# Gate and up products of a feed-forward layer by seven block products in place of eight

## The chip, the cores and the metric

The kernel runs on one core of one Trainium2 chip. The metric is the device time of one execution in microseconds (us). Before the change it is 2055.05 us, the median of three runs (2053.92 to 2055.37).

## The reference, cut to what matters

One cross-attention layer and one gated feed-forward layer, each with a layer norm ahead and a residual sum behind. The first takes 1190 us of the span and is not changed. The second works on 1600 tokens (16 x 100) of width 512 and a hidden width of 4096, with 4-bit weight codes and one scale per 32 inputs:

```python
xt = layernorm(x).reshape(1600, 512)
Wg, Wu, Wd = (lut[codes] * scales for gate, up, down)       # (4096, 512), (4096, 512), (512, 4096)
gate = einsum('th,nh->tn', xt, Wg)
up   = einsum('th,nh->tn', xt, Wu)
gelu = tanh(0.79788 * (gate + 0.044715 * gate**3)) * gate * 0.5 + gate * 0.5
out  = x + einsum('tn,hn->th', gelu * up, Wd)
```

## The kernel before, in words

Every float32 operand of a large product is kept as a pair of rounded halves (`_hi`, `_lo`), and a product is three matmuls: hi x hi, lo x hi, hi x lo (`matmul3`, L318 for each of them). A `_hi` half is made by a cast on ScalarE (L660), the `_lo` half by a subtraction on VectorE (L891) or GpSimd.

The feed-forward hidden width is cut into `JT` = 16 slices of 256 columns (index jt), the tokens into `NCHUNK` = 4 chunks of 400 (index ch). One step m is one slice and one chunk:

- `gate_up(m)`: for each half z of 128 hidden columns, `half(m, z, 0)` (gate) and `half(m, z, 1)` (up), 12 matmuls of 128x400 each over four blocks of 128 inputs: 48 matmuls. n = 2m + z numbers the halves.
- per n: ScalarE squares the gate values out of PSUM (L780) and scales them (L782), VectorE multiplies by the gate (`argument`, L1089), ScalarE takes tanh (L788), VectorE does `gelu` (L1097) and `gated` (L1104), each with one operand in PSUM; ScalarE casts `inter_hi` (L660), GpSimd subtracts `inter_lo` (L1357).
- `down(m)`: four output blocks of 6 matmuls, 24 in all, each added to the residual sum in SBUF by VectorE (`down_add`, L1118).

TensorE issues gate_up(m), then down(m-1), 72 matmuls a step. Gate and up use PSUM banks 0 to 3, down uses banks 4 to 7. Each engine works through its own list in order and waits on semaphores.

The codes of the next slice are turned into weights meanwhile, in six pieces of 128x512 (gate, up, down, two nibbles each): VectorE `decode` (two TENSOR_SCALAR, L1075 and L1077, and one TENSOR_TENSOR, L1080, all SBUF to SBUF in int16), GpSimd `decode_scaled` (L1339), ScalarE `decode_hi` (L660), GpSimd `decode_lo` (L1346). `decode` of a piece waits until `decode_scaled` of the piece two before is done, since there are two `value` buffers. `pieces_at` sets the place of each piece in the steps. The weights of two slices have room side by side.

## Time and profile before

| | |
|---|---|
| median of three runs | 2055.05 us |
| profiled execution: its time | 2053.49 us |
| profiled execution: span | 2051.7 us |
| TensorE busy | 2022.6 us (99%) |
| VectorE busy | 1420.0 us (69%) |
| ScalarE busy | 967.8 us (47%) |
| GpSimd busy | 913.8 us (45%) |
| granted TensorE clock, mean | 0.998 |

Times in the profile are microseconds from the span's start. A busy time of TensorE is made of matmuls that overlap: one of 128x400 is listed with about 0.34 us, but the next starts 0.18 us after it. For how fast TensorE works, starts are compared, not durations. In the rows PE is TensorE, DVE is VectorE, ACT is ScalarE, POOL is GpSimd, and L318 is line 318 of the kernel.

### The profile page before, as it was taken

The numbers are of one execution on the slowest core, as the hardware profiler recorded it, in microseconds if no ns is written. First come the engines' busy times: TensorE is split into PE (matmuls) and PEld (weight loads), VectorE is DVE, ScalarE is ACT, GpSimd is POOL, SyncE is SP. The second block draws the span as 40 slices with busy tenths as digits, with TensorE's granted clock in tenths as the row PEclk, the third lists the DMA queues.
The fourth block names the chain that finished last, engine by engine and source line by source line (L and its number), as shares of the span: only waits on it lengthen the run. The fifth ranks groups of instructions, "written<-read, shape, count | busy, mean of one in ns | idle before, by whom it ended". The sixth has DMA issues, their size and how long they took to land.

```text
span 2051.7 us, 33236 instructions
## 1 busy us (share of the span) xinstructions
PE 2022.6 (99%) x11840; PEld 1951.7 (95%) x11840; DVE 1420.0 (69%) x2938; ACT 967.8 (47%) x2126; POOL 913.8 (45%) x1041
## 2 busy tenths in 40 slices
PE   6999999999999999999999999999999999999999
PEld 5899999999999999999999999999999999999999
DVE  6777777778877787877887977555555555555554
ACT  4555455555555555555555544333333333333332
POOL 6756655533444333344233345444444444444441
PEclk9999999999999999999999999999999999999999
DMA  6335344332333324233233241001000000000001
GB/s 185 131 108 171 124 132 130 129 107 87 128 107 96 126 86 140 84 112 118 81 111 116 95 160 45 31 32 31 32 31 31 32 31 32 31 31 31 1 1 65
DMA packets 91763, 172.05 MB, mean 84 GB/s; under 512 B 13056, under 2 KB 48016, under 8 KB 89552
## 3 DMA queue, kind: packets, MB, share of 16 engines
q1 hardware_dynamic: 91600, 169.93, 25.3%
q8 instruction: 96, 1.57, 0.3%
q14 instruction: 67, 0.55, 0.1%
HBM read 136.55 MB, written 33.36 MB: 83 GB/s over the span
## 4 chain that ended last, share of the span: by engine, by line
PE 94%; DVE 3%; ACT 1%; POOL 1%; issue 1%; DMA 0%; SPq 0%; POOLq 0%; DVEq 0%; ACTq 0%
PE psum L318 70%; PE psum L351 6%; PE psum L383 3%; PE psum L375 3%; PE psum L398 3%; PE psum L404 3%; PE psum L399 3%; PE psum L448 2%; DVE kaT_lo L891 1%; PE psum L414 1%; DVE work L997 0%; PE psum L419 0%; DMA xb<-in_x 0%; DVE yT_lo L891 0%; DVE k_ss L947 0%
## 5 line engine op out<-in xcount | busy, mean ns | idle before, releaser
L1089 DVE TENSOR_TENSOR sq<-psum,sq 128x400 f32<-128x400 f32 x128 | 73.5, 574 | 266.9 <-ACT sq L782 266.9
L891 DVE TENSOR_TENSOR kaT_lo<-psum,kaT_hi 128x488 fp32r<-128x488 f32 (+2 forms) x384 | 216.0, 613 | 51.8 <-ACT kaT_hi L660 51.8
L720 ACT ACTIVATE work<-psum,stats,q_rstd 100x361 f32<-100x361 f32 x256 | 163.8, 651 | 184.1 <-DVE stats L988 184.1
L318 PE MATMUL psum<-wk,ctxT_hi 128*122 128x512 f32 x768 | 242.8, 398 | 2.2 <-DVE wk L891 2.2
L1357 POOL TENSOR_TENSOR inter_lo<-act,inter_hi 128x400 fp32r<-128x400 f32 x128 | 136.9, 1070 | 186.9 <-ACT inter_hi L660 186.9
L660 ACT CAST kaT_hi<-psum 128x488 fp32r<-128x488 f32 (+2 forms) x384 | 178.9, 539 | 73.3 <-PE psum L383 72.3
L1276 POOL TENSOR_TENSOR k_ss<-k_ss,power 122x4 f32<-122x4 f32 x192 | 194.0, 1010 | 16.0
L978 DVE TENSOR_REDUCE stats<-psum 100x2 f32<-100x722 f32 x128 | 115.7, 904 | 106.1 <-PE psum L351 106.1
L780 ACT ACTIVATE sq<-psum 128x400 f32<-128x400 f32 x128 | 64.7, 505 | 247.8 <-PE psum L318 247.8
L318 PE MATMUL psum<-xT_hi,up_lo 128*128 128x400 f32 x512 | 176.9, 346 | 0.0
L318 PE MATMUL psum<-xT_hi,gate_hi 128*128 128x400 f32 x512 | 176.2, 344 | 0.7 <-DVE act L1104 0.7
L318 PE MATMUL psum<-xT_lo,up_hi 128*128 128x400 f32 x512 | 176.6, 345 | 0.0
L318 PE MATMUL psum<-xT_lo,gate_hi 128*128 128x400 f32 x512 | 176.6, 345 | 0.0
L318 PE MATMUL psum<-xT_hi,gate_lo 128*128 128x400 f32 x512 | 176.5, 345 | 0.0
L318 PE MATMUL psum<-inter_lo,down_hi 128*128 128x400 f32 x512 | 176.0, 344 | 0.0
L318 PE MATMUL psum<-xT_hi,up_hi 128*128 128x400 f32 x512 | 176.0, 344 | 0.0
L318 PE MATMUL psum<-inter_hi,down_lo 128*128 128x400 f32 x512 | 175.6, 343 | 0.0
L318 PE MATMUL psum<-inter_hi,down_hi 128*128 128x400 f32 x512 | 174.9, 342 | 0.0
L318 PEld LDWEIGHTS psum<-wk,ctxT_hi 128*122 128x122 f32 x768 | 140.2, 184 | 34.1 <-issue 2.4
L1274 POOL TENSOR_SCALAR k_ss<-k_ss 122x4 f32<-122x4 f32 x192 | 37.3, 195 | 300.4 <-DVE k_ss L947 299.7
L318 PE MATMUL psum<-xlnT_hi,head_w 128*128 128x400 f32 x512 | 150.1, 354 | 3.0 <-DVE xlnT_lo L891 1.8
L318 PE MATMUL psum<-wk,ctxT_lo 128*122 128x512 f32 x384 | 152.1, 396 | 0.0
(146 smaller groups left out, 5580.2 us busy)
## 6 DMA issues: line engine op xcount, KB each, us to landing
head_w<-spill_sq SPq DMA_DIRECT2D x48, 512.0 KB, 3.4
head_w<-spill_so SPq DMA_DIRECT2D x46, 512.0 KB, 3.8
wk<-spill_sk SPq DMA_DIRECT2D x12, 1024.0 KB, 5.2
wv<-spill_sv SPq DMA_DIRECT2D x48, 256.0 KB, 2.8
spill_sq<-head_w SPq DMA_DIRECT2D x16, 512.0 KB, 3.0
spill_so<-head_w SPq DMA_DIRECT2D x16, 512.0 KB, 3.0
wk_raw<-in_ctxT SPq DMA_DIRECT2D x12, 361.0 KB, 4.0
head_raw<-in_Wq SPq DMA_DIRECT2D x16, 256.0 KB, 3.7
```

The costliest lines, as they stand in the source:

```text
L318: last = e.matmul(out, a_, b_, start=i == 0, stop=i == len(passes) - 1)
L351: last = e.matmul(bank[3 + h][0:SQ, 0:SCOLS], qT[quad % 2][h][q_][:, qs], kT[k_][:, h, 0:SCOLS], start=term == 0, stop=term == 2)
L375: last = e.transpose(bank[t][:, cols(h, KP)], khat[:, t, cols(h, HD)], ident[0:KP, 0:KP])
L383: last = e.transpose(bank[3 + t][0:KN[t], cols(h, SQ)], attn[h][:, t * KP:t * KP + KN[t]], ident[0:SQ, 0:SQ])
L660: e.copy(dst, src).then_inc(S[sem], 1)
L720: e.activation(attn[h][:, 0:SKV], bank[3 + h][0:SQ, 0:SKV], ACT.Exp, bias=st[:, h:h + 1], scale=rq[:, i * QH + h:i * QH + h + 1], accum_ou ...
L780: e.activation(sq[:, :], gate_bank(n), ACT.Square, scale=1.0 / CODE).then_inc(S["g2"], 1)
L891: e.tensor_tensor(dst, src, high.bitcast(F32), ALU.subtract).then_inc(S[sem], 1)
L978: e.tensor_reduce(st[:, 2 * p:2 * p + 2], scored(p), AX_X, ALU.max, negate=True).then_inc(S["mx"], 1)
L1089: e.tensor_tensor(sq[:, :], gate_bank(n), sq[:, :], ALU.mult).then_inc(S["arg"], 1)
L1276: e.tensor_tensor(c, c, power[0:KP, :], ALU.pow).then_inc(S["krs"], 1)
L1357: e.tensor_tensor(il[:, :], gact[n % 2][:, :], ih[:, :].bitcast(F32), ALU.subtract).then_inc(S["il"], 1)
```

## The change

Slice 0 is computed as before. For the 15 other slices two chunks of tokens are taken together as a pair p (h = p % 2 is 0 for chunks 0 and 1, 1 for chunks 2 and 3; two pairs a slice). The product of gate (and of up) is seen as 2x2 blocks: two halves of the hidden columns, two halves of the inputs, two chunks. Seven block products of 6 matmuls give what eight gave. They use sums of weight blocks (S1 to S4, made anew for every slice) and sums of token blocks (T1 to T4, made once and kept in SBUF). Three PSUM banks for gate and three for up (roles a, b, c) gather them; two are left for down, used in turn.

```diff
+PAIRS = 2 * (JT - 1)
+PRODUCTS = (("a", "A11", "B11"), ("b", "A12", "B21"), ("a", "S2", "T2"), ("c", "S1", "T1"), ("a", "S3", "T3"),
+            ("c", "S4", "B22"), ("a", "A22", "T4"))
...
+            def product(p, k, i):
...
+                if i == 0:
+                    e.wait_ge(S["gelu" if k == 0 else "inter"], before + 1 if p > 0 else (7, 8)[k])
...
+                elif i == 1 and k == 0:
+                    e.wait_ge(S["gelu"], before + 3)
...
+                elif i == 6:
+                    e.wait_ge(S[("gadd", "uadd")[k]], 3 * p + 2)
...
+            for p in range(PAIRS):
+                for at in range(2 * NP):
+                    product(p, at % 2, at // 2)
+                    if p == 0 and 3 <= at < 7:
+                        down(12 + at - 3)
+                    elif p > 0 and 3 <= at < 11:
+                        down(8 + 8 * p + at - 3)
```

TensorE adds each product into a bank (`role_bank`). ScalarE copies a running bank out (`evict`, six copies a pair), VectorE adds the copy to another bank (`combine`, six a pair). For hidden block n + 1 of a pair both gate and up values then lie in SBUF, for n + 2 the up values do. The two ScalarE passes of the polynomial become one (`square`):

```diff
+            def evict(p, k, w):
...
+                e.copy(kept[k][w][:, :], role_bank(k, p, "aac"[w])).then_inc(S[("gev", "uev")[k]], 1)
+            def combine(p, k, w):
...
+                e.tensor_tensor(dst, src, kept_, ALU.add).then_inc(S[("gadd", "uadd")[k]], 1)
-                e.activation(sq[:, :], sq[:, :], ACT.Copy, bias=GELU_C, scale=GELU_A * GELU_C).then_inc(S["poly"], 1)
...
-                e.tensor_tensor(sq[:, :], gate_bank(n), sq[:, :], ALU.mult).then_inc(S["arg"], 1)
+                e.scalar_tensor_tensor(out=gact[n % 3][:, :], in0=gact[n % 3][:, :], scalar=1.0 / GELU_A, in1=gate_source(n), op0=ALU.add,
+                                       op1=ALU.mult).then_inc(S["arg"], 1)
```

Weights: GpSimd writes the scaled gate and up codes to a float32 stage, makes four sums of 128x256 for each (`weight_sums`), and the 14 blocks in use are cast (`block_hi`, ScalarE) and subtracted (`block_lo`, GpSimd) one by one, each after its block's last use. Codes have one buffer in place of two. Tokens: for h = 0 VectorE makes the sums (`token_sums`), for h = 1 GpSimd does, from reloads of the normalised tokens (`load_raw`) and from chunk 3 put together again (`rebuild`); all this stands between step 3 and pair 1. In pair 0 `decode` of four pieces of slice 2 follows on VectorE.

On VectorE, a stretch in which pieces are decoded: before, in a step of slice 1 (L1089 argument, L1075 to L1080 one piece, L1097 gelu, L1104 gated, L1118 the down sums).

```order
L1089 TENSOR_TENSOR sq0<-psum,sq0 128x400
L1075 TENSOR_SCALAR value0<-up_packed0 128x512
L1077 TENSOR_SCALAR mag<-up_packed0 128x512
L1080 TENSOR_TENSOR value0<-value0,mag 128x512
L1097 SCALAR_TENSOR_TENSOR act0<-tanh0,psum 128x400
L1104 SCALAR_TENSOR_TENSOR act0<-act0,psum 128x400
```

After, in the middle of a pair with h = 0 (L1280 to L1285 one piece, L1331 a down sum, L1319 combine, L1293 argument).

```order
L1285 TENSOR_TENSOR value1<-value1,mag 128x512
L1331 SCALAR_TENSOR_TENSOR x1T1<-psum,x1T1 128x400
L1280 TENSOR_SCALAR value0<-up_packed 128x512
L1282 TENSOR_SCALAR mag<-up_packed 128x512
L1285 TENSOR_TENSOR value0<-value0,mag 128x512
L1331 SCALAR_TENSOR_TENSOR ysum<-psum,ysum 128x400
L1280 TENSOR_SCALAR value1<-up_packed 128x512
L1282 TENSOR_SCALAR mag<-up_packed 128x512
L1285 TENSOR_TENSOR value1<-value1,mag 128x512
L1319 TENSOR_TENSOR gate_kept2<-psum,gate_kept2 128x400
L1331 SCALAR_TENSOR_TENSOR ysum<-psum,ysum 128x400
L1293 SCALAR_TENSOR_TENSOR g1<-g1,gate_kept2 128x400
```

Four pieces now stand ahead of the combine that opens hidden block n + 1, where one piece stood between two operations of a hidden block, and the argument behind it has both operands in SBUF.

On GpSimd, a slice being prepared: before, a piece of down and the work around it (L1339 scaling, L1357 inter_lo, L1346 the low half).

```order
L1339 TENSOR_TENSOR wide0<-value0,down_scale0 128x512
L1357 TENSOR_TENSOR inter2_lo<-act0,inter2_hi 128x400
L1346 TENSOR_TENSOR down0_lo<-wide0,down0_hi 128x512
L1339 TENSOR_TENSOR wide1<-value1,down_scale0 128x512
L1357 TENSOR_TENSOR inter3_lo<-act1,inter3_hi 128x400
L1346 TENSOR_TENSOR down0_lo<-wide1,down0_hi 128x512
```

After, in a pair with h = 1, from inter_lo of n on (L1706 inter_lo, L1677 block_lo, L1647 scaling, L1659 the low half of down).

```order
L1706 TENSOR_TENSOR inter4_lo<-g0,inter4_hi 128x400
L1677 TENSOR_TENSOR gate0_lo<-gate_stage,gate0_hi 128x2x128
L1677 TENSOR_TENSOR up0_lo<-up_stage,up0_hi 128x2x128
L1677 TENSOR_TENSOR gate0_lo<-gate_stage,gate0_hi 128x2x128
L1677 TENSOR_TENSOR up0_lo<-up_stage,up0_hi 128x2x128
L1647 TENSOR_TENSOR wide0<-value0,down_scale 128x512
L1677 TENSOR_TENSOR gate_sums_lo<-gate_stage_sums,gate_sums_hi 128x256
L1677 TENSOR_TENSOR up_sums_lo<-up_stage_sums,up_sums_hi 128x256
L1647 TENSOR_TENSOR wide1<-value1,down_scale 128x512
```

The second scaling of down now stands behind six block subtractions and the first scaling.

On GpSimd in pair 0 (L1684 rebuild, L1690 to L1696 token_sums, L1666 to L1671 weight_sums); the list before has nothing like it between slices 0 and 1.

```order
L1684 TENSOR_TENSOR raw2<-xT3_hi,xT3_lo 128x400
L1690 TENSOR_TENSOR raw0<-raw1,raw0 128x400
L1692 TENSOR_TENSOR raw1<-raw2,raw1 128x400
L1694 TENSOR_TENSOR raw2<-raw2,raw0 128x400
L1696 TENSOR_TENSOR raw3<-raw3,raw2 128x400
L1647 TENSOR_TENSOR gate_stage<-value0,gate_scale 128x2x256
L1647 TENSOR_TENSOR gate_stage<-value1,gate_scale 128x2x256
L1666 TENSOR_TENSOR gate_stage_sums<-gate_stage 128x256
```

Token sums now come ahead of the first scaling for slice 2, on which a VectorE decode waits.

## Rows read from the trace of the kernel before

**Rows 1.** The page: busy time by engine, and the chain that ended last by engine.
```profile
PE 2022.6 (99%) x11840; PEld 1951.7 (95%) x11840; DVE 1420.0 (69%) x2938; ACT 967.8 (47%) x2126; POOL 913.8 (45%) x1041
...
PE 94%; DVE 3%; ACT 1%; POOL 1%; issue 1%; DMA 0%; SPq 0%; POOLq 0%; DVEq 0%; ACTq 0%
```
**Rows 2.** The chain in order of time: start, length, what.
```profile
1234.65 814.06 PE psum L318 x4476
```
**Rows 3.** Busy us of each engine in 52 us of the feed-forward layer, with counts.
```profile
1345.00:1397.00 52.00, 52.00 (x288) 52.00 (x287) 28.79 (x58) 19.52 (x38) 22.51 (x20) 1.00 0.10 32
```
**Rows 4.** Groups by line, 1250 to 2051.7: count | busy, mean ns | idle before.
```profile
L1357 POOL TENSOR_TENSOR inter_lo<-act,inter_hi 128x400 fp32r<-128x400 f32 x122 | 129.1, 1058 | 164.6 <-ACT inter_hi L660 164.6
L1118 DVE SCALAR_TENSOR_TENSOR ysum<-psum,ysum 128x400 f32<-128x400 f32 x184 | 102.3, 571 | 44.1 <-PE psum L318 44.1
...
L788 ACT ACTIVATE tanh<-sq 128x400 f32<-128x400 f32 x122 | 65.7, 538 | 78.2 <-DVE sq L1089 78.2
...
L660 ACT CAST inter_hi<-act 128x400 fp32r<-128x400 f32 x122 | 64.3, 527 | 157.5 <-DVE act L1104 157.5
L780 ACT ACTIVATE sq<-psum 128x400 f32<-128x400 f32 x121 | 61.1, 505 | 237.6 <-PE psum L318 237.6
L1346 POOL TENSOR_TENSOR up_lo<-wide,up_hi 128x512 fp32r<-128x512 f32 x30 | 39.2, 1307 | 88.2 <-ACT up_hi L660 88.2
...
L1339 POOL TENSOR_TENSOR wide<-value,up_scale 128x512 f32<-128x512 f16 x30 | 35.6, 1187 | 0.0
...
L660 ACT CAST up_hi<-wide 128x512 fp32r<-128x512 f32 x30 | 18.2, 605 | 2.9 <-POOL wide L1339 2.9
```
**Rows 5.** Groups by line, whole run: the one GpSimd subtraction of 256 columns.
```profile
L1331 POOL TENSOR_TENSOR wv<-wv_raw,wv 128x256 fp32r<-128x256 f32 x16 | 11.9, 742 | 1.3
```
**Rows 6.** Timeline 1509 to 1512: hand-overs, and a piece decoded beside an idle GpSimd.
```profile
1509.30 0.34 PE L318 MATMUL psum<-xT_hi,gate_lo 128*128 128x400 f32 x1
1509.48 0.34 PE L318 MATMUL psum<-xT_hi,up_hi 128*128 128x400 f32 x1
...
1509.68 0.51 ACT L780 ACTIVATE sq<-psum 128x400 f32<-128x400 f32 x1 [4.07 <-PE psum L318]
...
1511.28 0.42 DVE L1075 TENSOR_SCALAR value<-down_packed 128x512 int16<-128x512 int16 x1
...
1511.61 0.42 DVE L1077 TENSOR_SCALAR mag<-down_packed 128x512 int16<-128x512 int16 x1
...
1512.07 0.42 DVE L1080 TENSOR_TENSOR value<-value,mag 128x512 int16<-128x512 int16 x1
...
1512.41 0.56 DVE L1097 SCALAR_TENSOR_TENSOR act<-tanh,psum 128x400 f32<-128x400 f32 x1
```
**Rows 7.** Timeline 1250 to 1254: a piece decoded while GpSimd has work.
```profile
1250.68 1.51 POOL L1346 TENSOR_TENSOR gate_lo<-wide,gate_hi 128x512 fp32r<-128x512 f32 x1 [0.73 <-ACT gate_hi L660]
1251.13 1.35 DVE L1075 TENSOR_SCALAR value<-up_packed 128x512 int16<-128x512 int16 x1
1252.15 1.35 POOL L1339 TENSOR_TENSOR wide<-value,up_scale 128x512 f32<-128x512 f16 x1
1252.40 1.39 DVE L1077 TENSOR_SCALAR mag<-up_packed 128x512 int16<-128x512 int16 x1
...
1253.82 0.43 DVE L1080 TENSOR_TENSOR value<-value,mag 128x512 int16<-128x512 int16 x1
1254.16 0.56 DVE L1097 SCALAR_TENSOR_TENSOR act<-tanh,psum 128x400 f32<-128x400 f32 x1
```
**Rows 8.** Timeline 1199 to 1202: a VectorE subtraction from SBUF beside a GpSimd one.
```profile
1199.03 1.83 DVE L891 TENSOR_TENSOR xT_lo<-xT_lo,xT_hi 128x1600 fp32r<-128x1600 f32 x1 [0.68 <-ACT xT_hi L660]
...
1199.50 2.29 POOL L1357 TENSOR_TENSOR inter_lo<-act,inter_hi 128x400 fp32r<-128x400 f32 x1 [10.40 <-ACT inter_hi L660]
```
**Rows 9.** Timeline of GpSimd: the first scaling for slice 1.
```profile
1244.63 1.17 POOL L1339 TENSOR_TENSOR wide<-value,gate_scale 128x512 f32<-128x512 f16 x1 [0.36 <-DVE value L1080]
```
**Rows 10.** The page: a DMA issue of 256 KB; a token block's reload is 200 KB.
```profile
wv<-spill_sv SPq DMA_DIRECT2D x48, 256.0 KB, 2.8
```

More of the change, by code:

```diff
@@ L64 @@
 d_xi0 d_xi1 d_xi2 xTh xTl d_y0 d_y1 d_y2
-d_c0 d_c1 dec scaled wh wl
-gate up g2 poly arg tanh gelu inter ih il down yadd
+d_c0 d_c1 d_c2 dec scaled wh wl
+gate up g2 arg tanh gelu inter ih il down yadd
+gprod uprod gev uev gadd uadd sums bh bl dh dl d_r rebuilt tokens th tl
 d_o0 d_o1 d_o2 d_o3
@@ L839, in scalar_program @@
             u = UNITS - 1
-            polynomial(0)
+            square(0)
             for h in range(QH):
@@ L843, in scalar_program @@
             tangent(0)
-            polynomial(1)
+            square(1)
             transposed_attn(u)
@@ L851, in scalar_program @@
             inter_hi(1)
-            polynomial(2)
+            square(2)
             for h in range(QH):
@@ L859, in scalar_program @@
             inter_hi(2)
-            polynomial(3)
+            square(3)
             tangent(3)
@@ L863, in scalar_program @@
             inter_hi(3)
-            polynomial(4)
+            square(4)
             norm3_hi(1)
@@ L868, in scalar_program @@
             norm3_hi(3)
-            polynomial(5)
+            square(5)
             tangent(5)
@@ L872, in scalar_program @@
             inter_hi(5)
[L873 to L887 removed]
+            for j in range(4):
+                token_hi(0, 0, j)
@@ L1248, in vector_program @@
             gated(5)
-            down_add(0)
+            for q in range(4):
+                down_add(q)
             decode(PIECES)
-            down_add(1)
+            for q in range(4, 8):
+                down_add(q)
             decode(PIECES + 1)
-            for m in range(3, STEPS):
-                for z in range(2):
-                    n = 2 * m + z
-                    argument(n)
-                    for piece in pieces_at(m, z):
-                        decode(piece)
-                    gelu(n)
-                    gated(n)
-                down_add(m - 1)
@@ L1263, in vector_program, with coming_piece @@
-            down_add(STEPS - 1)
+            token_sums(0)
+            argument(6)
+            decode(PIECES + 2)
+            for j in range(4):
+                token_lo(0, 0, j)
+            gelu(6)
+            gated(6)
+            decode(PIECES + 3)
+            token_sums(1)
+            argument(7)
+            for j in range(4):
+                token_lo(0, 1, j)
+            gelu(7)
+            gated(7)
+            for q in range(8, 12):
+                down_add(q)
+            def coming_piece(p, d):
+                jt, h = p // 2 + 1, p % 2
+                if jt + 1 < JT and d < (4, 2)[h]:
+                    decode(PIECES * (jt + 1) + 4 * h + d)
@@ L1265, in gpsimd_program @@
+            n = block_index(PAIRS, 0)
+            gelu(n - 2)
+            argument(n - 1)
+            gated(n - 2)
+            gelu(n - 1)
+            gated(n - 1)
+            for d in range(8):
+                down_add(8 + 8 * PAIRS + d)
         def gpsimd_program(e):
@@ L1460, in gpsimd_program @@
                 inter_lo(n)
+            e.wait_ge(S["out"], 4 * NQ)
+            e.wait_ge(S["nT2"], NG * GB)
             decode_scaled(PIECES)
[L1462 removed]
             decode_scaled(PIECES + 1)
[L1465 to L1474 removed]
+            weight_sums(1, 0)
```

594 lines of the change are left out of this document (464 added, 130 removed).

## The prediction

> **What bounds the kernel now.** I read the page first: TensorE is busy for 99% of the span and holds 94% of the chain that ended last [rows 1]. Then the chain in order of time: from 1234.65 on it is one piece, 4476 matmuls in 814.06 us [rows 2], so one every 0.1819 us, with no wait. Then the busy times of a stretch: in 52 us VectorE works 28.8, ScalarE 19.5, GpSimd 22.5 [rows 3]. The granted clock there is 1.00, the level of 2.4 GHz. Last the groups and three timelines for the durations. The feed-forward layer is bound by the number of matmuls, and the others have slack. The question is whether they keep it.
>
> **What goes.** A step has 48 gate and up matmuls; 15 slices of 4 steps have 2880; seven for eight leaves 2520. 360 x 0.1819 = 65.5 us [rows 2]. A pair has 132 matmuls in place of 144: 24.0 us, in 22 slots of 6 matmuls, 1.09 us each. Slots 0 to 3 are gate and up of products 0 and 1, slot 4 is the first down (d0), 6 the second (d1), 18 the last (d7), 20 and 21 are product 6.
>
> **What comes, as load.** Per slice (48.0 us, two pairs), taken start to start, which for a 0.57 us sum is about 0.50:
> - VectorE: 28.8 of 52 us is 29.0 a slice [rows 3]. 12 combines at the price of a down sum [rows 4] add 6.0: 35.0 of 48.0, undisturbed.
> - ScalarE: 12 copies at 0.505 in (6.1), 8 polynomial passes at 0.538 out (-4.3), 4 casts of 512 out (-2.4), 14 casts of 256 in. Casts of 512 and 400 take 0.605 and 0.527 [rows 4], by that line 0.43, so 6.0: 19.7 + 5.4 = 25.
> - GpSimd: 4 subtractions of 1.307 out [rows 4], 8 sums and 14 block subtractions of 0.742 in [rows 5]: 22.7 - 5.2 + 16.3 = 33.8.
> Each alone fits. So the sum of busy times says that TensorE stays the bound; the loops between the engines say otherwise.
>
> **Two engines that hold each other up.** A decoding piece takes 1.13 us when GpSimd is idle (0.33 + 0.46 to the third start, then 0.34 to what follows) [rows 6]. With GpSimd at work it took from 1251.13 to 1254.16, 3.0 us: the first operation ended 0.5 us after gate_lo, lasted 1.35 in place of 0.42, the second lasted 1.39 and outlasted the scaling that had got in between [rows 7]. They took turns, whole operations each. It happens with float32 too: a 400-column subtraction on GpSimd, 1.06 alone [rows 4], took 2.29 beside a VectorE subtraction from SBUF and ended 0.93 after it [rows 8]. The Trainium skill says the same in "SBUF — State Buffer" (Who interferes with whom): a two-port operation, or one with two SBUF inputs, and a GpSimd operation exclude each other for the whole instruction. By that rule the argument, gelu and gated of block n + 1 and the gated of n + 2, which now read two SBUF tiles, join those that wait; before they read PSUM. No row of before shows these four, but rows 8 has the same kind of read in a subtraction. I charge three on the path 0.3 us each (from 0 to a whole 0.74 block operation).
>
> **The loop of a half slice.** Hand-overs cost about 0.2 us from TensorE (last gate matmul issued 1509.30, the next group 1509.48, square at 1509.68 [rows 6]) and some 0.03 elsewhere. From the end of d1's sum on VectorE, at about slot 8:
> 1. h = 0. Four pieces and three down sums, undisturbed 4 x 1.13 + 3 x 0.50 = 6.0. GpSimd does inter_lo, two scalings, four sums and a third scaling in the same time. Taken in turn, VectorE waits for what is left of them: 0.5, 0.6, 0.6, then 0.7, 0.7, 0.2, 0.7, 1.1, together 5.1. With the combine: 11.6.
>    h = 1. ScalarE can't square block n + 1 before both casts of down and two block casts. On GpSimd stand one inter_lo (1.0), six blocks (4.1), two scalings (2.3), with six decode operations of 0.37 in between (2.2); then ScalarE's 0.55 + 0.8. About 11.
> 2. From that square to inter_lo of n + 2, one after the other: 0.51 square, 0.87 argument, 1.05 combine and sum (tanh hidden), 0.87 gelu, 0.87 gated, 0.53 cast, 0.51 square, 0.57 argument, 0.54 tanh, 0.51 square of n + 3, 0.57, 0.54, 0.45 copy, 0.53 cast, 1.06 inter_lo: 10.0.
> 3. d0 of the next pair waits for that inter_lo; d1's sum ends three slots, 0.2 and 0.57 later: 4.0.
> Sum 25.6 (h = 0), and with 0.7 for block casts among the squares 25.7 (h = 1), against 24.0. TensorE waits about 1.6 us a pair, at d0, d7 or product 1. Slices 1 to 14 prepare a successor: 14 pairs with h = 1 and 13 with h = 0 (pair 0 is counted below): 27 x 1.6 = 43 us. Its ends: 0 if the turns don't fall together (then loop 1 is 6.5 and 24.0 holds), 3.6 if each of the twelve decode operations waits for half a scaling (7.1 in place of 5.1); I take the middle since the queue's own order gives it.
>
> **The passage from slice 0 to pair 1.** The stage lies where attention's tiles were, so scaling for slice 1 starts as before at about 1244.6 [rows 9]. Without waits pair 0 would begin at 1258.7 (1234.65 + 132 matmuls of steps 2, 3 and downs 0 to 2) and d0 of pair 1 at 1282.7. Followed through the queues:
> - GpSimd's scaling of up stands behind inter_lo 6, which waits for VectorE's four token sums, a decode and four token subtractions, about 0.5 each and 0.7 more for a turn. Scaling then ends at 1262.4. Four sums, token sums in turn with them, casts: product 0 at 1269.5. inter_lo 7 frees the first down at 1273.3, due 1263.0: 10.3 us.
> - Ten block subtractions (7.0), two rebuilds and four sums (6 x 1.06) follow; ScalarE's third copy stands behind their casts: product 5 at 1287.6 in place of 1284.2: 3.4 us.
> - inter_lo, two scalings, rebuild, four sums, two more scalings (13 us) bring GpSimd to 1299.6. VectorE's third piece waits for the first of these, and combine for the fourth piece: product 6 at 1304.0, due 1289.8: 14.2 us. The reloads (about 2.8 us each as in [rows 10], issued during the rebuild) are hidden by this.
> - The remaining chain to gelu of n + 2, with four token casts and subtractions in it: 3.3, and 2.0 for inter_lo behind the down halves.
> Sum 33 us. At least 20 (the first two and half of the third), at most 45 (each token operation a full turn).
>
> **The end.** The last 8 downs can only start when block n + 2 is split: 2.5 us after product 6; before, the last downs had others ahead of them. The attention part keeps its order; only a tile's place moves: 0.
>
> **Sum.** -65.5 + 43 + 33 + 2.5 = +13. The profiled execution took 2053.5 (span 2051.7 and 1.8 around it), so 2066.5; the runs' median lies 1.6 higher: **2068 us**.
>
> **Rivals.**
> - *TensorE stays the bound* once pair 1 runs: the load sums above are for it (35 of 48 on VectorE), and turns only happen if both have work at the moment; in slice 2 and later of before a piece hardly waits. The pieces stood beside an idle GpSimd there (its 22.5 of 52 [rows 3]), which is against. Then 2055 - 65.5 + 33 + 2.5 = 2025; with a short passage as well, down to 1992.
> - *Slower by a dearer form.* The Trainium skill, "Vector Engine (DVE) Microarchitecture Reference" (Points that are easy to get wrong), says that a scalar_tensor_tensor with two float32 SBUF sources runs at half rate. No run here shows it. The mechanism in this kernel: the four operations a pair that lost their PSUM source stand in loop 2, at 0.57 if priced as the down sum, at about 1.06 if priced as the nearest two-SBUF row, GpSimd's [rows 4]. 4 x 0.49 x 27 = 53 us on top: 2121. It decides as soon as the loop and not TensorE sets the pace.
> - *The clock.* If waits of 10 to 14 us let the granted clock fall to 1.2 GHz for part of the passage, it costs a few us more; it stays 1.00 over all of rows 3, and I give it nothing.
> - *It doesn't do what it says*: 360 matmuls are gone from TensorE's list and the rest keep their shape, so no.
>
> **How the numbers follow.** Forecast 0.50 (own range 2045 to 2092), TensorE the bound 0.35 (of this 0.08 near 1992), the dearer form 0.12, others 0.03. The range 2015 to 2105 leaves out most of 1992 and 2121. Within 0.2% (4 us) of 2055 no change can be told. Faster takes 0.34 and the low tail of the forecast, 0.06: 0.40; same 0.08; slower 0.52.
>
> **What would show it.** TensorE's start distance within a product stays 0.18 us. Busy TensorE falls below 95% after 1260, with waits of 0.5 to 2 us at the down matmuls (released by inter_lo or the down sum) once or twice a pair, and a pair takes 25.6 us. Decoding operations last 0.8 us or more on the mean in place of 0.42 to 0.6. Between 1258 and 1320 TensorE stands for some 33 us, the longest wait at product 6 of pair 0, released by a combine. The four operations with kept tiles take 0.57 plus a turn. Wrong is the forecast if a pair takes 24.0 us from slice 2 on, or if the passage costs under 20 us.

## The result, and the profile after

The changed kernel took 2062.9 us (median of 7 runs, 2060.3 to 2063.5), the kernel before 2055.4 (7 runs, 2052.5 to 2055.9). The ratio is 1.0037, 95% interval 1.0025 to 1.0049: slower by 0.4%. The forecast was 2068 us, with a chance of 0.52 for slower. The profiled execution has a span of 2061.7 us, 10.0 more than before.

The page of the kernel after, busy time by engine and chain by engine (before: [rows 1]):
```profile
PE 1972.7 (96%) x11480; PEld 1886.8 (92%) x11480; DVE 1654.6 (80%) x3142; ACT 1015.2 (49%) x2344; POOL 1137.8 (55%) x1323
...
PE 73%; DVE 14%; POOL 5%; issue 5%; ACT 3%; DMA 1%; SPq 0%; DVEq 0%; ACTq 0%; POOLq 0%
```
TensorE has 360 matmuls less, and its part of the chain fell from 94% to 73%: it is no longer the engine that everything waits for. VectorE has 235 us more and GpSimd 224. The chain now runs through VectorE for a seventh of the span although VectorE is idle for a fifth of it.

The busy times of 50 us of the loop, the columns as in [rows 3]:
```profile
1380.00:1430.00 50.00, 48.37 (x265) 47.44 (x264) 43.34 (x71) 22.56 (x52) 36.88 (x39) 1.00 0.10 32
```
TensorE is short of full by 3%. By slice (d0 to d0 of the pair after next) the time is 50.2 us where the matmuls alone need 48.0. The timeline of TensorE, its only rows with idle time between 1600 and 1651:
```profile
1600.27 0.42 PE L373 MATMUL psum<-inter_hi,down_hi 128*128 128x400 f32 x1 [0.90 <-POOL inter_lo L1706]
...
1615.91 0.42 PE L373 MATMUL psum<-inter_hi,down_hi 128*128 128x400 f32 x1 [0.24 <-DVE ysum L1331]
...
1625.44 0.42 PE L373 MATMUL psum<-inter_hi,down_hi 128*128 128x400 f32 x1 [0.55 <-POOL inter_lo L1706]
...
1650.49 0.42 PE L373 MATMUL psum<-inter_hi,down_hi 128*128 128x400 f32 x1 [0.89 <-POOL inter_lo L1706]
```
Three waits a slice: d0 behind h = 1 (0.90), d7 in h = 0 (0.24), d0 behind h = 0 (0.55). They are where the prediction put them. The difference of 2.2 us is more than their sum of 1.69. Each wait costs about 0.2 us that no row shows as idle: the matmul with the 0.24 starts 0.57 us after the one before it, where 0.18 is the rule, and the next one 0.26 after that.

The passage, all of TensorE's waits up to the first down of pair 1:
```profile
1269.34 0.67 PE L712 MATMUL psum<-xT_hi,gate_hi 128*128 128x400 f32 x1 [9.00 <-POOL gate_lo L1677]
...
1287.38 0.45 PE L712 MATMUL psum<-xT_hi,gate_sums_hi 128*128 128x400 f32 x1 [0.88 <-ACT gate_kept L902]
...
1309.32 0.70 PE L712 MATMUL psum<-xT_hi,gate_hi 128*128 128x400 f32 x1 [19.50 <-DVE gate_kept L1319]
...
1318.51 0.45 PE L712 MATMUL psum<-xT_hi,gate_hi 128*128 128x400 f32 x1 [2.39 <-DVE g L1298]
...
1323.34 0.42 PE L373 MATMUL psum<-inter_hi,down_hi 128*128 128x400 f32 x1 [2.38 <-POOL inter_lo L1706]
```
And the end: one wait of 2.46 us ahead of the last downs, as forecast 2.5.

Where 10.0 us come from, by stages of the two profiled executions:

| | forecast | measured |
|---|---|---|
| matmuls gone | -65.5 | -65.5 |
| unchanged part ahead of product 0 (its last matmul over at 1260.2 in place of 1258.7) | 0 | +1.5 |
| passage from there to d0 of pair 1 (1323.34), 24.0 without waits, 63.1 measured | +33 | +39.1 |
| 27 pairs, 24.0 without waits, 25.14 measured (1323.34 to 2002.02) | +43 | +30.6 |
| wait at the end | +2.5 | +2.5 |
| the rest; up to 1.4 of it a lower clock in the last downs | 0 | +1.8 |
| sum | +13 | +10.0 |

The +1.5 isn't a cost of the change. In the twelve profiled executions of changed kernels the same instructions end anywhere between 1257.6 and 1262.0, so stretches behind them are counted from their end and not from the span's start. A pair with h = 0 took 25.2 us and one with h = 1 25.0 (forecast 25.6 and 25.7).

The groups by line from 1345 to 2000: count, then busy us and mean ns, then idle before. Decoding and the two-tile operations:
```profile
L1285 DVE TENSOR_TENSOR value<-value,mag 128x512 int16<-128x512 int16 x78 | 66.2, 848 | 2.7
...
L1310 DVE SCALAR_TENSOR_TENSOR g<-g,up_kept 128x400 f32<-128x400 f32 x53 | 43.3, 817 | 0.9
...
L1310 DVE SCALAR_TENSOR_TENSOR g<-g,psum 128x400 f32<-128x400 f32 x52 | 29.7, 571 | 1.8
...
L1280 DVE TENSOR_SCALAR value<-gate_packed 128x512 int16<-128x512 int16 x26 | 27.1, 1042 | 0.0
L1282 DVE TENSOR_SCALAR mag<-down_packed 128x512 int16<-128x512 int16 x26 | 24.9, 958 | 0.0
...
L1298 DVE SCALAR_TENSOR_TENSOR g<-g,gate_kept 128x400 f32<-128x400 f32 x26 | 23.5, 905 | 0.0
```
A decode operation that took 0.42 beside an idle GpSimd [rows 6] takes 0.72 to 1.04 on the mean, by kind; only the second one of the gate pieces keeps 0.41. The same line L1310 takes 571 ns when it reads PSUM and 817 when both sources are in SBUF. GpSimd pays as well:
```profile
L1677 POOL TENSOR_TENSOR gate_lo<-gate_stage,gate_hi 128x256 fp32r<-128x256 f32 x53 | 53.0, 1000 | 0.0
...
L1677 POOL TENSOR_TENSOR up_sums_lo<-up_stage_sums,up_sums_hi 128x256 fp32r<-128x256 f32 x40 | 29.5, 738 | 0.0
```
The undisturbed price of this operation is 0.74 [rows 5], and up_sums_lo, which meets little, has it.

### The profile page after: what moved, and what is told of

The parts are those of the page before. It is cut to its first block, busy times and chain, and to the rows that moved or that the text cites. A ratio compares the mean times of both kernels' runs of the same rounds, so it can differ in the third digit from the quotient of the medians.

```text
span 2061.7 us, 34434 instructions
## 1 busy us (share of the span) xinstructions
PE 1972.7 (96%) x11480; PEld 1886.8 (92%) x11480; DVE 1654.6 (80%) x3142; ACT 1015.2 (49%) x2344; POOL 1137.8 (55%) x1323
## 3 DMA queue, kind: packets, MB, share of 16 engines
q1 hardware_dynamic: 93328, 172.39, 25.7%
## 4 chain that ended last, share of the span: by engine, by line
PE 73%; DVE 14%; POOL 5%; issue 5%; ACT 3%; DMA 1%; SPq 0%; DVEq 0%; ACTq 0%; POOLq 0%
PE psum L373 39%; PE psum L712 10%; PE psum L406 6%; PE psum L430 3%; PE psum L453 3%; PE psum L438 3%; PE psum L459 3%; PE psum L454 3%; DVE value L1280 3%; DVE mag L1282 2%; PE psum L503 2%; POOL inter_lo L1706 1%; DVE value L1285 1%; DVE g L1298 1%; DVE g L1293 1%
## 5 line engine op out<-in xcount | busy, mean ns | idle before, releaser
L1706 POOL TENSOR_TENSOR inter_lo<-g,inter_hi 128x400 fp32r<-128x400 f32 x128 | 135.3, 1066 | 188.0 <-ACT inter_hi L759 186.9
L373 PE MATMUL psum<-inter_hi,down_hi 128*128 128x400 f32 x512 | 180.0, 352 | 26.6 <-POOL inter_lo L1706 21.0
L1586 POOL TENSOR_TENSOR q_sqs_lo<-q_sq,q_sqs_hi 128x400 fp32r<-128x400 f32 x60 | 63.0, 1050 | 158.6 <-ACT q_sqs_hi L759 158.5
L373 PE MATMUL psum<-oT_hi,head_w 128*128 128x400 f32 x496 | 145.8, 355 | 2.6 <-POOL head_w L1617 2.6
L759 ACT CAST yT_hi<-psum 128x400 fp32r<-128x400 f32 x128 | 63.1, 493 | 161.2 <-PE psum L459 161.2
L453 PE MATMUL psum<-kaT_hi,ctxN_hi 122*128 122x400 f32 (+1 forms) x384 | 135.4, 353 | 5.3 <-DVE kaT_lo L1096 4.5
L1331 DVE SCALAR_TENSOR_TENSOR ysum<-psum,ysum 128x400 f32<-128x400 f32 x192 | 106.5, 563 | 40.2 <-PE psum L373 40.1
L373 PEld LDWEIGHTS psum<-inter_hi,down_hi 128*128 128x128 f32 x512 | 96.9, 189 | 39.7 <-issue 39.5
L454 PE MATMUL psum<-kaT_hi,ctxN_lo 122*128 122x400 f32 (+1 forms) x384 | 132.6, 345 | 0.0
L1159 DVE TENSOR_TENSOR work<-psum,k_ss 122x512 f32<-122x512 f32 x192 | 125.3, 679 | 4.0 <-POOL k_ss L1573 3.9
```

The costliest lines, as they stand in the source:

```text
L373: last = e.matmul(out, a_, b_, start=i == 0, stop=i == len(passes) - 1)
L453: e.matmul(out, nh[0:n, t, cs], aT[0][0:n, t, :], start=t == 0, stop=False)
L454: e.matmul(out, nl[0:n, t, cs], aT[0][0:n, t, :], start=False, stop=False)
L759: e.copy(dst, src).then_inc(S[sem], 1)
L1159: e.tensor_tensor(khat[:, t, :].rearrange("p (h d) -> p h d", h=QH), bank[t][0:KP, :].rearrange("p (h d) -> p h d", h=QH), k_ss[u % 2][:, ...
L1706: e.tensor_tensor(il[:, :], gact[n % 3][:, :], ih[:, :].bitcast(F32), ALU.subtract).then_inc(S["il"], 1)
```

## The experiments

Eleven kernels ran. "Slice" below is the distance of two waits of the same kind, or of two first downs, one slice apart, in the steady part; 48.0 is TensorE without a wait, and the steady part has 13.5 slices. Each kernel was timed beside runs of the kernel before, whose medians lie between 2053.2 and 2055.4, so the ratios compare better than the times.

### The missed queue: x1_codes_early
The long wait at product 6 ends with the fourth decoded piece, and VectorE had stood still before the first of them. From the timeline of VectorE in the kernel after:
```profile
1298.95 0.45 DVE L1280 TENSOR_SCALAR value<-gate_packed 128x512 int16<-128x512 int16 x1 [7.23 <-DMA gate_scale<-in_gate_scales]
```
The codes and scales of slice 2 are issued by SyncE behind the last reload of token blocks, which waits until a buffer is read out. The edit lets the first two loads go ahead:
```
-            for h in range(2):
-                for r in range(2):
-                    load_raw(h, r)
+            load_raw(0, 0)
+            load_raw(0, 1)
+            load_codes(2, (0, 1))
+            load_raw(1, 0)
+            load_raw(1, 1)
+            load_codes(2, (2,))
```


> The changed kernel with one move on the SyncE queue: the gate and up codes of slice 2 are loaded ahead of the token reloads for h = 1, not behind them. In the changed kernel VectorE waited 7.2 us for these codes in pair 0, ahead of a 19.5 us wait of TensorE. Theory A (the passage is set by GpSimd, where the third scaling stands behind the token sums; the code load only runs beside them): the third piece still waits for a scaling that can't come before the token sums end at about 1299, so product 6 of pair 0 comes 2 to 3 us sooner, about 2060. Theory B (the late code load is the cause): 7 us sooner, about 2056.

Measured: 2059.5 us (2057.4 to 2061.3), ratio 1.0022 (1.0012 to 1.0033). The row of product 6 in its timeline:
```profile
1306.40 0.70 PE L712 MATMUL psum<-xT_hi,gate_hi 128*128 128x400 f32 x1 [17.35 <-DVE gate_kept L1319]
```
d0 of pair 1 comes at 1320.44, 2.9 us sooner, but 1.5 of these lie in the unchanged part ahead of the passage. Counted from its end, d0 comes after 61.8 us in place of 63.1; in the seven kernels that have the early codes and the old passage it comes after 61.0 to 62.0. So taking away a wait of 7.2 us on VectorE gave back 1 to 2 us, since scaling by GpSimd was the next to be late (VectorE's third piece now waits 1.65 us for it). The medians are 3.4 us apart, and the intervals of the two ratios overlap; what would make up the rest wasn't found. The other kernels below that need it are built on this one.

### Moving the passage's work: x2_passage
On top of the early codes, two of the four pieces, the last token halves and the down halves go from pair 0 to pair 1 (on VectorE, ScalarE and GpSimd), for example on VectorE:
```
+                if p == 1:
+                    decode(PIECES * 2 + 2)
+                    decode(PIECES * 2 + 3)
...
-                coming_piece(p, 2)
+                if p > 1:
+                    coming_piece(p, 2)
```


> The codes-early kernel with the order of pairs 0 and 1 changed: VectorE's two up pieces of slice 2 move from pair 0 to pair 1, the last four token casts and subtractions move to the start of pair 1, GpSimd's scalings and weight sums for slice 2 move from pair 0 to pair 1, behind inter_lo of n + 3 and the halves of down. Nothing is left out. Theory A (order in the queues makes the passage long): product 6 of pair 0 at about 1294 in place of 1309, d0 of pair 1 at about 1305 in place of 1323, of which pair 1 gives 5 to 10 back: 2048 to 2055. Theory B (GpSimd simply has too much to do there, in whatever order): what pair 0 gains pair 1 gives back: 2059 to 2062.

Measured: 2062.9 us, ratio 1.0036 (1.0025 to 1.0048), the profiled execution 2059.9: nothing won. Its waits of TensorE in pair 0 and at the start of pairs 1 and 2:
```profile
1298.16 0.70 PE L712 MATMUL psum<-xT_hi,gate_hi 128*128 128x400 f32 x1 [9.61 <-DVE gate_kept L1319]
...
1312.52 0.67 PE L373 MATMUL psum<-inter_hi,down_hi 128*128 128x400 f32 x1 [6.13 <-POOL down_lo L1664]
...
1326.64 0.42 PE L373 MATMUL psum<-inter_hi,down_hi 128*128 128x400 f32 x1 [2.62 <-DVE ysum L1331]
...
1346.96 0.42 PE L373 MATMUL psum<-inter_hi,down_hi 128*128 128x400 f32 x1 [1.66 <-POOL inter_lo L1711]
```
Product 6 came 8.2 us sooner than in the run above and d0 of pair 1 7.9 us; from there to d0 of pair 2 it then had five waits, 6.7 us in all, and this d0, at 1346.96, is no sooner than in the run above (1346.49). This fits a passage that is bound by what VectorE and GpSimd have to do in it; one order other than the first doesn't prove it for all.

### Is it the two engines? x3_decode_thin and x4_gpsimd_thin
Both are built on the kernel after. In the first, the decode operations from the second prepared slice on write 16 columns in place of 512; in the second, GpSimd's block sums and halves work on 2 x 8 = 16 columns in place of 256. The number and order of instructions stay:
```
+                if jt > 1:
+                    val, codes, into = val[:, 0:16], codes[:, 0:16], mag[:, 0:16]
```
```
+                if jt > 1:
+                    wh, wl, of = (t[:, :, 0:8] for t in (wh, wl, of))
```


> The changed kernel in which VectorE's three decode operations work on 16 of 512 columns for slices 2 to 15 (the other codes are left out); all else stays. Theory A (loops through VectorE, made long by the decode pieces and their turns with GpSimd, cost 1.1 us a pair): the waits at d0 and d7 go, a pair takes 24.0 to 24.1 us, about 30 us less and 5 us less in pair 0, near 2028. Theory B (GpSimd's and ScalarE's own order sets d0 behind a pair with h = 1): the wait of 0.9 at d0 behind each h = 1 pair stays or only halves, near 2040.

> The changed kernel in which GpSimd's weight sums and block subtractions work on 16 of 256 columns for slices 2 to 15 (the rest of these sums and halves is left out); VectorE's and ScalarE's work stays whole. Theory A (turns between VectorE and GpSimd): decode operations come down to near 0.42, the gelu operations with two SBUF tiles to 0.57 to 0.7, and the pair to 24.0 us: near 2030. Theory C (VectorE's own length, without turns, sets the pace): a pair stays at 25.1 and the time at 2062. Theory D (two float32 SBUF sources halve the rate of scalar_tensor_tensor): these operations stay at 0.9 or more beside an idle GpSimd.

Measured, one execution each: 2030.9 and 2026.5 us. In both, TensorE has no wait between d0 of pair 1 and the one ahead of the last downs. So the loop's waits need the work of both engines: either one, made light, is enough to end them. Each edit takes plain work away as well as turns. What tells the two apart is VectorE in x4, where its own list is whole: in the 550 us from 1400 on it is busy for 448.0, which is 39.1 us a slice, in place of 43.5. These 4.4 us a slice were turns, and d7, which waits for VectorE's sum alone, lost its wait with them. For d0 behind h = 1 it stays open how much was turns, since the thinned blocks stand ahead of inter_lo in GpSimd's own queue.

Operations of VectorE in x4, where GpSimd is busy for half of the time (277.5 of 550 us) in place of three quarters:
```profile
L1280 DVE TENSOR_SCALAR value<-up_packed 128x512 int16<-128x512 int16 x24 | 30.3, 1263 | 0.0
L1285 DVE TENSOR_TENSOR value<-value,mag 128x512 int16<-128x512 int16 x70 | 29.8, 425 | 2.4
...
L1310 DVE SCALAR_TENSOR_TENSOR g<-g,up_kept 128x400 f32<-128x400 f32 x46 | 26.3, 572 | 0.8
...
L1293 DVE SCALAR_TENSOR_TENSOR g<-g,gate_kept 128x400 f32<-128x400 f32 x23 | 13.4, 581 | 1.5
```
The first operation of each piece still meets a scaling, and at 1.07 to 1.26 us on the mean it is longer than in the kernel after; the other two are at 0.41 to 0.44. At 0.57 and 0.58 the two-tile operations cost what the same operation costs with a PSUM source. The rival of the dearer form is out: the 817 to 905 ns of the kernel after are turns with GpSimd, not a rate. The half rate that the Trainium skill gives for two float32 SBUF sources ("Vector Engine (DVE) Microarchitecture Reference", Points that are easy to get wrong) isn't borne out here. What the Trainium skill says in "SBUF — State Buffer" (Who interferes with whom), that such an operation and one of GpSimd exclude each other, is: L1310 takes 571 ns with a PSUM source and 817 with two tiles in SBUF beside the same GpSimd.

### Is it the order? x5 to x7
Something in the traces did not fit a plain lack of time. Just ahead of the wait of 0.90, VectorE stands idle for ScalarE, and ScalarE has put a down cast and two block casts for the next slice ahead of the square. The timelines of VectorE and ScalarE in the kernel after:
```profile
1586.35 0.58 DVE L1319 TENSOR_TENSOR gate_kept<-psum,gate_kept 128x400 f32<-128x400 f32 x1 [0.26 <-PE psum L712]
1587.51 0.57 DVE L1331 SCALAR_TENSOR_TENSOR ysum<-psum,ysum 128x400 f32<-128x400 f32 x1 [0.58 <-PE psum L373]
1589.29 1.20 DVE L1293 SCALAR_TENSOR_TENSOR g<-g,gate_kept 128x400 f32<-128x400 f32 x1 [1.21 <-ACT g L923]
```
```profile
1587.58 0.62 ACT L759 CAST down_hi<-wide 128x512 fp32r<-128x512 f32 x1 [1.70 <-POOL wide L1647]
1588.11 0.40 ACT L759 CAST gate_sums_hi<-gate_stage_sums 128x256 fp32r<-128x256 f32 x1
1588.42 0.41 ACT L759 CAST up_sums_hi<-up_stage_sums 128x256 fp32r<-128x256 f32 x1
1588.72 0.54 ACT L923 ACTIVATE g<-gate_kept 128x400 f32<-128x400 f32 x1
```
The sum gate_kept was ready at 1586.93; its square came at 1588.72. Of these 1.8 us ScalarE spent 0.65 waiting for GpSimd's scaling of down, 0.53 on the down cast and 0.61 on the block casts. x5, built on the early codes like all that follow, changes only this:
```
+                square(n + 1)
                 if h == 1 and jt + 1 < JT:
                     down_hi(jt + 1, 1)
-                    for k in range(2):
-                        block_hi(jt + 1, k, 3)
-                square(n + 1)
                 tangent(n + 1)
                 if h == 1 and jt + 1 < JT:
-                    for k in range(2):
-                        block_hi(jt + 1, k, 4)
+                    for i in (3, 4):
+                        for k in range(2):
+                            block_hi(jt + 1, k, i)
```
x6 moves the casts of block 5 behind the last square, those of block 6 into the next pair, and GpSimd's halves of blocks 5 and 6 behind the last inter_lo of the slice, with the first scaling right behind them and so ahead of inter_lo of n:
```
+                if p > 0 and h == 0:
+                    for i in (5, 6):
+                        for k in range(2):
+                            block_lo(jt, k, i)
+                    if jt + 1 < JT:
+                        decode_scaled(PIECES * (jt + 1))
                 inter_lo(n)
```
x7 has both.

> Nothing is left out; the third slice's codes are queued early as in the run before (2059.5 us, ratio 1.0022), and in the pairs of h = 1 ScalarE takes the square of the second block ahead of the second down cast, and its tangent ahead of the four casts of blocks 3 and 4. In the trace VectorE's argument of that block waits 1.2 us for this square, once per slice. Theory A (the waits of TensorE behind a pair come from the order in which the evicting engines reach the second block, so 1.2 us won at the start of this chain removes the wait of 0.90 us behind h = 1): 14 waits x 0.9, about 12 us less, 2047 us. Theory B (the engines are short of time as such, whatever the order): within 2 us of 2059.5. Both at once would show as the wait shrinking by less than half.

> Nothing is left out; early codes again, and now only the other half is reordered. In the pairs of h = 0 VectorE begins the first decoding piece right behind the first argument (it stood idle 1.7 us there), and its sum for the second gate block comes ahead of the last step of the fourth piece. The casts and halves of weight blocks 5 and 6 move behind the last two block halves of the products (inter_lo), into a stretch in which GpSimd waited 3 us. Theory A (order): the waits behind h = 0, 0.23 and 0.53 us per slice, go, and inter_lo behind h = 1 starts up to 0.8 us sooner, so of the 0.90 most goes too: 14 x (0.76 + 0.6), 15 to 20 us less, about 2042 us. Theory B (time short as such, or the two engines only collide elsewhere): less than 4 us.

> Nothing is left out; both reorderings together, on the early codes. Theory A: no wait of TensorE in the steady pairs, 24.0 us each as where the decoding or GpSimd's halves were thinned: 27 x 1.13 = 30 us less than with the early codes alone, so about 2030 us, faster than the kernel before by 1.2%. Theory B: within 5 us of 2059.5, the same as before or slower. If only one of the two orders matters, it equals the better of the two.

The expectations of x6 and x7 speak of VectorE's order too. That was a mistake: their kernels hold only the move of the blocks and of the first scaling, VectorE's order is unchanged in them, and its half of the question had to wait for x8. Measured: x5 2046.3 us, ratio 0.9958 (0.9941 to 0.9975); x6 2052.2, 0.9989 (0.9980 to 0.9998); x7 2049.5, 0.9974 (0.9965 to 0.9983). TensorE's waits in a slice of x5:
```profile
1607.82 0.42 PE L373 MATMUL psum<-inter_hi,down_hi 128*128 128x400 f32 x1 [0.24 <-DVE ysum L1330]
...
1617.32 0.42 PE L373 MATMUL psum<-inter_hi,down_hi 128*128 128x400 f32 x1 [0.53 <-POOL inter_lo L1705]
```
and of x6:
```profile
1609.20 0.42 PE L373 MATMUL psum<-inter_hi,down_hi 128*128 128x400 f32 x1 [0.58 <-DVE ysum L1335]
...
1618.70 0.42 PE L373 MATMUL psum<-inter_hi,down_hi 128*128 128x400 f32 x1 [0.53 <-POOL inter_lo L1738]
```
The 0.90 behind h = 1 is gone in both. In x5 it is cured by one step earlier at the head of the chain, for 13.2 us against the 12 forecast. In x6 it is cured by less work ahead of inter_lo at its tail, but d7 waits 0.33 us longer. From GpSimd and VectorE in x6:
```profile
1599.73 1.23 POOL L1738 TENSOR_TENSOR inter_lo<-g,inter_hi 128x400 fp32r<-128x400 f32 x1
```
```profile
1597.30 0.42 DVE L1282 TENSOR_SCALAR value<-gate_packed 128x512 int16<-128x512 int16 x1
...
1599.98 1.27 DVE L1285 TENSOR_SCALAR mag<-gate_packed 128x512 int16<-128x512 int16 x1
```
The moved halves are over at 1596.7, before the first piece begins, so the 0.33 doesn't come from them. More likely it comes from inter_lo of n, which behind the first scaling meets the second piece: one step of it lasts 1.27 in place of 0.41. No run moves the scaling alone. x7 shows that the second cure adds nothing to the first and keeps its price.

### VectorE's order in h = 0: x8 to x11
In h = 0 VectorE works without a gap from its first piece to the last block; ahead of it, it stands idle:
```profile
1601.69 0.58 DVE L1331 SCALAR_TENSOR_TENSOR x1T<-psum,x1T 128x400 f32<-128x400 f32 x1 [1.20 <-PE psum L373]
...
1603.86 0.57 DVE L1331 SCALAR_TENSOR_TENSOR x1T<-psum,x1T 128x400 f32<-128x400 f32 x1 [0.51 <-PE psum L373]
1604.35 0.97 DVE L1280 TENSOR_SCALAR value<-gate_packed 128x512 int16<-128x512 int16 x1
```
x8, on x5, fills that gap with the first piece and takes the sum for the second gate block and the sixth down sum in between the steps of the last piece (a piece's three steps can now be issued apart). On GpSimd the first scaling moves ahead of inter_lo of n, so that it follows this piece. VectorE's list:
```
+                    decode(first)
+                    down_add(q)
+                    gelu(n)
+                    gated(n)
+                    down_add(q + 1)
+                    decode(first + 1, (0,))
+                    down_add(q + 2)
+                    decode(first + 1, (1, 2))
+                    decode(first + 2, (0,))
+                    down_add(q + 3)
+                    decode(first + 2, (1, 2))
+                    down_add(q + 4)
+                    decode(first + 3, (0, 1))
+                    combine(p, 0, 1)
+                    down_add(q + 5)
+                    decode(first + 3, (2,))
+                    argument(n + 1)
```
x9 is x8 with the passage of x2; x10 is x8 with ScalarE's old order; x11 is x8 with only the first piece moved: the other pieces whole, no down sum between their steps, the sum for the second gate block behind all four.

> Nothing is left out. Base: the run in which only ScalarE's order was changed (2046.3 us, waits left per slice: 0.24 for ysum before d7 and 0.53 for inter_lo before d0, both in or behind h = 0). In that run VectorE is busy without a gap from its first sum of the down products' stretch to the last block, and stood idle 1.4, 0.5, 0.5 and 0.5 us in the stretch ahead of it. Here, in h = 0, the first piece is decoded right behind the first argument, the adds are spread between the steps of the pieces, and the second gate block's sum comes ahead of the last step of the fourth piece. (The two runs that were to test this earlier held only the move of blocks 5 and 6; the order of VectorE was unchanged in them.) Theory A (a slice is held up by VectorE's time in the pairs of h = 0, and what it stood idle there can be used): both waits go, 14 x 0.77 = 11 us less, 2035 us. Theory B (what is started sooner only meets GpSimd sooner and is slowed by it, work of the two is what it takes): less than 3 us, 2044 to 2047 us.

> Nothing is left out. The run above, and with it the passage of the earlier run: two of the second slice's four pieces and the last token halves go from pair 0 to pair 1. Alone this gave nothing (2062.9 against 2059.5), pair 1 having given back what pair 0 won. Theory A (it was given back since the steady order had no time to spare; with the new order it has): 4 to 8 us below the run above. Theory B (the work of GpSimd up to pair 2 is the limit of the passage, whatever the order behind it): within 3 us of the run above, or longer.

> Nothing is left out. VectorE's new order in h = 0 (first piece behind the first argument, adds spread between steps) on the early codes, with ScalarE's order as it was. With both orders the time was 2031.1, with ScalarE's alone 2046.3, with neither 2059.5. Theory A (each half of a slice has its own late chain, each cured by its own order): the waits in and behind h = 0 go, the 0.90 behind h = 1 stays, 2059.5 - 14 x 0.77 = about 2048 us. Theory B (the second half only inherits what the first is late): all go, 2031 us. Theory C (it needs ScalarE's order first): 2056 to 2060.

> Nothing is left out. The fastest kernel so far (2031.1), in which now only the first piece and its scaling stand ahead; the sum for the second gate block is again behind the whole fourth piece, and the adds stand whole between the pieces. Theory A (what counts is the time that VectorE stood idle ahead of the pieces, about 1.7 us, filled by the first piece): 2031 us, within 2. Theory B (what counts is the place of the sum and of the sixth down sum in the queue): d7 waits 0.2 us for ysum again and d0 some tenths, 2034 to 2045 us.

| kernel | time, us | ratio to before (95%) | waits left in a slice | slice, us |
|---|---|---|---|---|
| after | 2062.9 | 1.0037 (1.0025 to 1.0049) | 0.90, 0.24, 0.55 | 50.2 |
| x1 codes early | 2059.5 | 1.0022 (1.0012 to 1.0033) | 0.89, 0.23, 0.53 | 50.2 |
| x6 blocks late | 2052.2 | 0.9989 (0.9980 to 0.9998) | 0.58, 0.53 | 49.6 |
| x7 x5 and x6 | 2049.5 | 0.9974 (0.9965 to 0.9983) | 0.57, 0.53 | 49.4 |
| x5 ScalarE's order | 2046.3 | 0.9958 (0.9941 to 0.9975) | 0.24, 0.53 | 49.2 |
| x10 VectorE's order | 2044.1 | 0.9953 (0.9937 to 0.9970) | 0.95 | 49.0 |
| x11 x5, first piece | 2039.1 | 0.9930 (0.9916 to 0.9945) | 0.31 | 48.6 |
| x8 x5 and x10 | 2031.1 | 0.9883 (0.9869 to 0.9898) | none | 48.0 |
| x9 x8, passage of x2 | 2032.4 | 0.9889 (0.9872 to 0.9905) | none | 48.0 |

x8 is faster than the kernel before by 1.2% and than the kernel after by 1.5%, with nothing left out. The busy times of the kernel after, of x5 and of x8 in the steady part:
```profile
1400.00:1950.00 550.00, 532.62 (x2899) 522.79 (x2898) 476.86 (x767) 248.82 (x570) 405.66 (x417) 1.00 0.10 33
```
```profile
1400.00:1950.00 550.00, 541.47 (x2952) 532.09 (x2951) 489.76 (x784) 254.93 (x575) 413.44 (x425) 1.00 0.10 33
```
```profile
1400.00:1950.00 550.00, 549.90 (x3026) 546.75 (x3025) 470.65 (x803) 265.43 (x593) 422.51 (x433) 1.00 0.11 33
```
TensorE is full in x8. By slice VectorE works 43.5 us in the kernel after, 43.8 in x5 and 41.1 in x8, GpSimd 37.0, 37.0 and 36.9. So x5 ended the wait behind h = 1 with VectorE's and GpSimd's work as long as before, and there the order alone is what changed. The new order in h = 0 did two things: it filled the gap, and it shortened VectorE's work by about 2.5 us a slice, for which fewer turns are the only reason, as the operations are the same. No run here parts the two. Single operations of x8:
```profile
L1288 DVE TENSOR_TENSOR value<-value,mag 128x512 int16<-128x512 int16 x78 | 55.3, 709 | 2.2
L1313 DVE SCALAR_TENSOR_TENSOR g<-g,up_kept 128x400 f32<-128x400 f32 x54 | 48.9, 905 | 0.9
```
The last step of a piece takes 709 ns in place of 848; up_kept's operation is even slower than before (905 against 817), and it does no harm. The first piece, now in a gap of GpSimd, is at its undisturbed price, and so is the second, with 0.42 for each of its steps:
```profile
1634.26 0.42 DVE L1281 TENSOR_SCALAR value<-gate_packed 128x512 int16<-128x512 int16 x1
1634.59 0.42 DVE L1284 TENSOR_SCALAR mag<-gate_packed 128x512 int16<-128x512 int16 x1
1635.04 0.43 DVE L1288 TENSOR_TENSOR value<-value,mag 128x512 int16<-128x512 int16 x1
```
x10 says that the two halves of a slice have chains of their own: its three waits became one, the untouched 0.95 behind h = 1. x11 says that the filled gap is not all: without the spread steps and the sum ahead of the last one, 0.3 us is left at d0 behind h = 0, while d7 waits no more. x9 gains as little as x2: product 6 comes at 1299.6 in place of 1305.6, and pair 1 gives it back.

## Why the prediction was right, and where it was not

**The sign and the mechanism** held. It said that TensorE would leave the role of the bound though each engine's load fits into 48 us, and that the waits would stand at d0 and d7, released by inter_lo and the down sum, because VectorE and GpSimd hold each other up. The rows of the kernel after show the places. x3 and x4 show that the waits need the work of both, and x4 that the turns are real: 4.4 us a slice on VectorE.

**The steady loops** were taken as 1.6 us a pair and are 1.13, 30.6 for 43 us: a size, within the ends that were given (0 and 3.6). In h = 0 the stretch from d1's sum to the combine took 10.9 us against 11.6, so, with the same 6.5 for the undisturbed operations, the turns in it took 4.4 and not 5.1. In h = 1 the stretch up to the square took 9.3 against 11, and the chain from there to inter_lo 11.3 against 10.7. The mechanism was told too narrowly, too. The prediction gave the turns as the whole reason, but x5, with VectorE as busy as before, lost its wait behind h = 1, and x8 has most of the turns and no wait. What costs is a turn that falls on a late chain, and what made the chains late was as much the order of the queues: a down cast, which itself waited for GpSimd, and block casts ahead of a square, and 1.7 us of idle VectorE ahead of its longest stretch. The text had named the first ("ScalarE can't square block n + 1 before both casts of down and two block casts") and priced it as part of the load, where it could be had for nothing.

**The passage** was taken as 33 and is 39.1. The step that failed: "The reloads ... are hidden by this". GpSimd, which was to be through with the two scalings for slice 2 at 1299.6, was through at 1303.7. It had stood 1.48 us until VectorE freed the buffers and then for the last reload:
```profile
1294.79 1.02 POOL L1690 TENSOR_TENSOR raw<-raw 128x400 f32<-128x400 f32 x1 [0.97 <-DMA raw<-spill_x2T]
```
What stands behind the reloads in SyncE's queue, the codes and scales of the next slice, isn't hidden either: it held VectorE for 7.23 us. From product 5 to product 6 it took 21.9 us where 16.4 were forecast. x1 gives back 1 to 2 us of that.

Products 0 and 5 were forecast at 1269.5 and 1287.6 and came at 1269.3 and 1287.4. That is luck: the passage itself began 1.5 us later than in the kernel before, and counted from its beginning they came after 9.2 and 27.2 us, not 10.8 and 28.9. Product 6 was forecast after 45.3 and came after 49.1. The other part is the clock, which the prediction gave nothing.

**The clock.** After the wait of 9.00 us the matmuls start 0.33 us apart:
```profile
1269.81 0.54 PE L712 MATMUL psum<-xT_lo,gate_hi 128*128 128x400 f32 x1
1270.14 0.54 PE L712 MATMUL psum<-xT_hi,gate_lo 128*128 128x400 f32 x1
```
That is the level of 1.2 GHz in place of 2.4; the granted clock from 1269 to 1272 is 0.50. There are some 24 such starts up to d0 of pair 1, 11 in the head of pair 1 and 9 in the last downs, after the wait of 2.46: at 0.15 us more each 3.6, 1.6 and 1.4 us at most, of which the first part is hidden where the next product waits anyway, and the second lies in the row of the 27 pairs. Two windows with such stretches, where the third number from the end is the granted clock:
```profile
1309.00:1330.00 21.00, 15.92 (x64) 15.20 (x65) 15.86 (x26) 11.65 (x27) 12.93 (x13) 0.80 0.08 26
2048.00:2058.00 10.00, 9.85 (x46) 9.64 (x47) 3.85 (x7) 0.07 (x1) 1.04 (x1) 0.83 0.28 104
```
TensorE's waits in the passage add up to 34.2 of the 39.1 us, so about 5 are slower or later starts. How much the passage would be shorter at the full clock was not measured by an experiment.

**The rivals.** TensorE as the bound (2025, or 1992 with a short passage) came true in another kernel: x8's 2031.1 is 2055 - 65.5 and some 41 for the passage and the end. The dearer form is refuted by x4. The forecast's errors cancel in part: it had 12 us too much in the loops, 6 too little in the passage and nothing for 3 us elsewhere, half of which is where the profiled execution happened to stand ahead of product 0. The median came 5 us below it with less right than it looks.

**What stays open.** x8 still pays 37 us between the end of the unchanged part and d0 of pair 1. x2 and x9 show that moving two pieces and their scalings to pair 1 doesn't help; whether token sums and rebuilds could be made cheaper was not tried. The unchanged part alone differs by up to 4.4 us between profiled executions, so a few us of difference between two kernels with one execution each say nothing by themselves. Whether x8 gained in h = 0 by the filled gap or by the shorter turns is open.

## What to carry to other kernels

Taking matmuls away from a full TensorE is only worth it if the engines around it can be queued so that each chain of evictions starts as soon as its input is there; load sums of 73% (VectorE) and 70% (GpSimd) did not show the loss, a walk along the queues did. When TensorE waits a few tenths of a microsecond at the same place in every round, look upstream in the same round for an engine that stood idle or did work that nobody needed yet, and move that before buying time elsewhere: two such moves gave 28 us, more than the change had lost. A queue that only issues transfers is a queue as well: what stands behind a guarded transfer waits with it.
